# Decoder layer with eight routed experts: gate and up weights become the loaded operand and are fetched from DRAM once per tile of rows

## The reference

```python
logits = xt @ Ws + bs                       # 1600 x 8
topk_w, topk_idx = jax.lax.top_k(logits, K) # K = 2 of E = 8 experts
topk_w = jax.nn.softmax(topk_w, axis=-1)
g = jnp.einsum('td,edf->tef', xt, Wg)       # D = 256, F = 688
u = jnp.einsum('td,edf->tef', xt, Wu)
h = jax.nn.silu(g) * u
y = jnp.einsum('tef,efd->ted', h, Wd)
out = jnp.einsum('ted,te->td', y, combine)  # combine holds the two weights of a row
x = layernorm(x + out)
```

## Time and profile before

| | |
|---|---|
| three timed runs | 719.72 us median (718.25 to 720.38) |
| the profiled execution | 723.84 us, of which the span of the trace is 721.9 us |
| PE busy | 645.6 us (89%) in 5190 instructions |
| PEld busy | 494.8 us (69%) |
| DVE, ACT, POOL busy | 381.0, 315.6, 287.8 us |
| DMA | 73.95 MB, 102 GB/s over the span; q1 65.53 MB, q0 7.61 MB |
| granted TensorE clock | 0.951 of 2.4 GHz on the mean |

### The profile page before, as it was taken

How to read it: one execution, slowest core, us unless ns; L and a number is a source line. 1 busy time by engine, 2 the same in 40 slices (tenths; PEclk the granted TensorE clock), 3 DMA queues, 4 the chain that set the end, 5 groups by cost and what they waited for, 6 DMA issues and landing times. The chain is left out here.

```text
span 721.9 us, 15610 instructions
## 1 busy us (share of the span) xinstructions
PE 645.6 (89%) x5190; PEld 494.8 (69%) x5191; DVE 381.0 (53%) x975; ACT 315.6 (44%) x761; POOL 287.8 (40%) x522
## 2 busy tenths in 40 slices
PE   6988977999999989999899729999999999999960
PEld 5887855677777767777677516777777777777750
DVE  2878765777777866787677641222222222222214
ACT  2344333677777766777676512222222222222202
POOL 3435454433333376336742321334333333334323
PEclk9999986999999998999999958999999999999995
DMA  8232114455556556555555550111221122112205
GB/s 255 76 77 73 55 34 125 130 167 163 169 170 173 160 152 188 167 163 163 145 147 144 186 214 23 26 31 28 33 36 30 30 31 35 29 30 30 28 1 182
DMA packets 60831, 73.95 MB, mean 102 GB/s; under 512 B 9498, under 2 KB 50786, under 8 KB 60002
## 3 DMA queue, kind: packets, MB, share of 16 engines
q1 hardware_dynamic: 54626, 65.53, 30.7%
q0 software_dynamic: 6144, 7.61, 6.5%
HBM read 38.38 MB, written 12.44 MB: 70 GB/s over the span
## 5 line engine op out<-in xcount | busy, mean ns | idle before, releaser
L1443 DVE TENSOR_REDUCE cmx<-ps 100x1 f32<-100x361 f32 x256 | 134.5, 531 | 69.5 <-PE ps L956 65.2
L1233 ACT ACTIVATE cpr<-ps 128x300 f32<-128x300 f32 x256 | 104.7, 419 | 57.6 <-PE ps L967 57.0
L1739 POOL DMA_INDIRECT accd<-y,si x32 | 51.3, 1602 | 137.4 <-DVE y L1962 137.4
L1950 DVE TENSOR_TENSOR hh<-sg,ps 128x344 f32<-128x344 f32 x64 | 32.8, 513 | 113.5 <-PE ps L1811 113.5
L956 PE MATMUL ps<-st 96*100 96x361 bf16 x256 | 85.7, 338 | 6.5 <-DMA st<-parts 3.1
L1833 PE MATMUL ps<-WD,hT 128*128 x384 | 88.3, 380 | 1.4 <-DVE y L1962 0.7
L1811 PE MATMUL ps<-WG,xsT 128*128 x256 | 86.3, 460 | 0.6 <-ACT xsT L1867 0.6
L1811 PE MATMUL ps<-WU,xsT 128*128 x256 | 85.6, 457 | 0.0
L967 PEld LDWEIGHTS ps<-st 120*128 120x128 bf16 x768 | 62.8, 102 | 31.6 <-issue 8.8
L1833 PEld LDWEIGHTS ps<-WD,hT 128*128 128x128 f32 x384 | 72.8, 190 | 16.1 <-issue 1.9
L967 PE MATMUL ps<-st 120*128 120x100 bf16 x768 | 76.8, 208 | 3.3 <-ACT st L1238 1.6
(11 more groups left out here) (219 smaller groups left out, 1104.7 us busy)
## 6 DMA issues: line engine op xcount, KB each, us to landing
st<-parts SPq DMA_DIRECT2D x192, 115.2 KB, 2.5
WD<-in_wd SPq DMA_DIRECT2D x6, 1024.0 KB, 11.5
cx<-in_ctxT SPq DMA_DIRECT2D x16, 361.0 KB, 5.1
WG<-in_wg SPq DMA_DIRECT2D x8, 688.0 KB, 4.7
WU<-in_wu SPq DMA_DIRECT2D x8, 688.0 KB, 4.5
x_sb<-in_x SPq DMA_DIRECT2D x8, 200.0 KB
x1d<-x SPq DMA_DIRECT2D x8, 200.0 KB
x1Td<-x1T SPq DMA_DIRECT2D x8, 200.0 KB, 3.3
```

The lines of the kernel that those rows point to most:

```text
L1233: act.activation(pr[:, h % (2 * HG), :], ps[:, B_T + h % 2, 0:NCH * L], ACT.Exp).then_inc(exp_ok, 1)
L1443: dve.tensor_reduce(mx[:, half, hh:hh + 1], ps[0:L, B_S + h % 2, 0:CTX], AX_X, ALU.max).then_inc(max_ok, 1)
L1739: pool.indirect_dma_start(accd, bass.IndirectOffsetOnAxis(ap=si[:, t.par:t.par + 1], axis=0), y[:, t.par, :], None, compute_op=ALU.add, bo ...
L1950: dve.tensor_tensor(hh[:, t.par, f * FH:(f + 1) * FH], sg[:, f, :], ps[:, B_U + f, 0:FH], ALU.mult).then_inc(h_ok, 1)
```

## The change

1. `WG` and `WU` are no longer in SBUF as a whole. On the host the columns of gate and up of an expert are laid out as 11 blocks of 128 (`ORDER`, `GU` = 1408 columns): gate 0 to 3, gate 4, a block that holds the last 48 columns of gate and (from column 64) of up, up 4, and up 0 to 3. SP fetches them from DRAM for each tile (`weights(t)`), 1.44 MB a time (two runs of 5632 bytes a partition), into one of four buffers `W`. The fetch for tile t waits until the gate and up products of tile t-4 are made, and reads the tile's expert from `expert_of` first. The buffer `W0` is filled with expert 0 in the cross-attention; one more POOL instruction on `r_jv` makes sure that tile 0 is expert 0's.
2. In `gate_up` the weights are the loaded operand and `xsT` streams past them, 128 columns each: 11 blocks x 2 chunks = 22 products, 44 PE instructions. The result has the hidden columns on the partitions, as `down` wants them, so `turn_hidden` and the two copies of `hT` are gone. The blocks come in three parts of 4, 3 and 4, each with its own bank for even and odd tiles. ACT makes one silu of 512 columns and two of 128, DVE two products of 128 and one of 512, straight into `hT`.
3. `WD` is fetched in the batches 0 to 5 of the cross-attention, `W0` in batch 6, in place of the pieces of `WG` and `WU`. Nothing but the stores is issued in its last turn.
4. The last norm comes in five pieces of 2, 3, 3, 3 and 2 slots of 128 rows (the last slot has 64). The root is taken by ACT (with a table load ahead of it), the reciprocal and the shift by DVE, POOL has no part in it. ACT applies slots 0 to 8, DVE slots 9 to 12.

```diff
-FH = F // 2
 FC = (F + P - 1) // P
 FP = FC * P
+FULL = F // P
+FLEFT = F - FULL * P
+U_AT = 64
+ORDER = ((("g", 0), ("g", 1), ("g", 2), ("g", 3)), (("g", 4), ("both", 5), ("u", 4)), (("u", 0), ("u", 1), ("u", 2), ("u", 3)))
+GU = P * sum(len(part) for part in ORDER)
...
-NQ = 4
-QT = TP // NQ
+PIECES = ((0, 2), (2, 5), (5, 8), (8, 11), (11, TP + 1))
+NQ = len(PIECES)
...
-                    for n in range(2 * E):
-                        if i == (n if n < E else n - 1):
-                            W, w = ((WG, wg), (WU, wu))[n % 2]
-                            sp.dma_start(W[:, :, n // 2, :], w[n // 2, :, :].rearrange("(k p) f -> p k f", p=P))\
-                                .then_inc(experts_in, 16)
+                    if 0 <= i < FC:
+                        sp.dma_start(WD[:, i, :, :], wd[:, i, :, :]).then_inc(R.wd_in, 16)
+                    if i == FC:
+                        sp.dma_start(W0[:, :, :], wgu[0, :, :, :]).then_inc(R.wd_in, 16)
...
-                    if i == NB - 1:
-                        for u in range(2):
-                            sp.wait_ge(kq_in[u], 16 * SLOTS * NB)
-                        sp.wait_ge(t_mm, H * (NB - 1))
-                        load_down(range(FC // 2))
...
-                    if i == NB - 1:
-                        load_down(range(FC // 2, FC))
...
-        hh = sb("hh", [P, 2, FP])
+        sg = sb("sg", [P, 6 * P])
+        W = [W0, *(sb(f"W{u}", [P, KC, GU]) for u in range(1, 4))]
...
+        def bank(t, part):
+            return 3 * t.par + part
...
+                def weights(t):
+                    wait(sp, gu_mm, 3 * (t.n - 3))
+                    e = sp.value_load(expert_of[0:1, bass.ds(t.n, 1)], min_val=0, max_val=E - 1)
+                    sp.dma_start(W[t.slot][:, :, :], wgu[bass.ds(e, 1), :, :, :].rearrange("e p k f -> p (e k) f"))\
+                        .then_inc(w_in[t.slot], 16)
+
+                def emit(t, n):
+                    if n == -1:
+                        weights(t + 2)
+                    if n + 3 < TILES:
+                        weights(t + 3)
...
-                def gate_up(t, e, halves):
+                def gate_up(t, parts):
                     pe.wait_ge(xT_ev, t.n + 1)
-                    for f in halves:
-                        wait(pe, h_ok, 2 * t.n + f - 1)
-                        for bank, W in ((B_G, WG), (B_U, WU)):
+                    wait(pe, w_in[t.slot], 16 * (t.lap + (t.slot > 0)))
+                    for part in parts:
+                        if part == 0:
+                            wait(pe, sg_ok, 2 * t.n - 3)
+                        else:
+                            wait(pe, h_ok, 2 * t.n - 4 + part)
+                        for i, (kind, _) in enumerate(ORDER[part]):
+                            c = i + sum(len(p) for p in ORDER[:part])
                             for k in range(KC):
-                                mm = pe.matmul(ps[:, bank + f, 0:FH], xsT[:, t.par, k, :],
-                                               W[:, k, bass.ds(e, 1), f * FH:(f + 1) * FH],
-                                               start=(k == 0), stop=(k == KC - 1))
-                            mm.then_inc(gu_mm, 1)
-
-                def turn_hidden(t):
-                    pe.wait_ge(h_ok, 2 * t.n + 2)
-                    wait(pe, hTa_ev, t.n)
-                    wait(pe, hTb_ev, t.n)
-                    for c in range(FC):
-                        mm = pe.transpose(ps[:, B_H + c // 4, c % 4 * P:(c % 4 + 1) * P],
-                                          hh[:, t.par, c * P:(c + 1) * P], ident[:, :])
-                        if c in (3, FC - 1):
-                            mm.then_inc(hT_mm, 1)
+                                mm = pe.matmul(ps[:, bank(t, part), i * P:(i + 1) * P], W[t.slot][:, k, c * P:(c + 1) * P],
+                                               xsT[:, t.par, k, :], start=(k == 0), stop=(k == KC - 1))
+                        mm.then_inc(gu_mm, 1)
...
                     for c in range(FC):
                         if c == 0:
-                            pe.wait_ge(hTa_ev, t.n + 1)
-                        if c == 4:
-                            pe.wait_ge(hTb_ev, t.n + 1)
+                            pe.wait_ge(h_ok, 2 * t.n + 2)
...
-                        turn_hidden(t - 1)
                     if n + 1 < TILES:
-                        coming = expert(t + 1)
-                        gate_up(t + 1, coming, (0,))
-                    if n == 1:
-                        pe.wait_ge(R.wd_in, 16 * FC)
+                        gate_up(t + 1, (0,))
                     if n >= 1:
                         down(t - 1, leaving)
                     if n + 2 < TILES:
                         turn_rows(t + 2)
                     if n + 1 < TILES:
-                        gate_up(t + 1, coming, (1,))
+                        gate_up(t + 1, (1, 2))
...
+                def silus(t, part):
+                    act.wait_ge(gu_mm, 3 * t.n + part + 1)
+                    wait(act, h_ok, 2 * t.n - part)
+                    if part == 0:
+                        a = act.activation(sg[:, 0:4 * P], ps[:, bank(t, part), :], ACT.Silu)
+                    else:
+                        act.activation(sg[:, 4 * P:5 * P], ps[:, bank(t, part), 0:P], ACT.Silu)
+                        a = act.activation(sg[U_AT:U_AT + FLEFT, 5 * P:6 * P], ps[0:FLEFT, bank(t, part), P:2 * P], ACT.Silu)
+                    a.then_inc(sg_ok, 1)
...
+                def hidden(t, part):
+                    dve.wait_ge(sg_ok, 2 * t.n + (2 if part == 1 else 1))
+                    dve.wait_ge(gu_mm, 3 * t.n + part + 1)
+                    if part == 1:
+                        wait(dve, y_mm, t.n - 1)
+                        left = slice(U_AT, U_AT + FLEFT)
+                        dve.tensor_tensor(hT[:, t.par, FULL - 1, :], sg[:, 4 * P:5 * P], ps[:, bank(t, part), 2 * P:3 * P], ALU.mult)
+                        h = dve.tensor_tensor(hT[left, t.par, FULL, :], sg[left, 5 * P:6 * P],
+                                              ps[left, bank(t, part), P:2 * P], ALU.mult)
+                    else:
+                        h = dve.tensor_tensor(hT[:, t.par, 0:FULL - 1, :].rearrange("p c t -> p (c t)"), sg[:, 0:4 * P],
+                                              ps[:, bank(t, part), :], ALU.mult)
+                    h.then_inc(h_ok, 1)
...
+                deviation(0)
+                deviation(1)
+                apply(0, (0, 1)).then_inc(res_ok, 1)
+                deviation(2)
+                apply(1, (2, 3, 4)).then_inc(res_ok, 1)
+                deviation(3)
+                apply(2, (5, 6))
+                deviation(4)
+                apply(2, (7,)).then_inc(res_ok, 1)
+                apply(3, (8,)).then_inc(res_ok, 1)
...
-                    last_stats(q)
+                    sums_of(q)
+                    if q >= 1:
+                        scales(q - 1)
+                    moments(q)
+                    if q >= 1:
+                        shifts(q - 1)
+                normal(9)
+                normal(10).then_inc(scaled_ok, 1)
+                scales(NQ - 1)
                 dve.wait_ge(rstd_ok, NQ)
-                for j in slots(NQ - 1):
-                    r = dve.tensor_scalar(acc[:, j, :], acc[:, j, :], mv[:, j, 0:1], rstd[:, j:j + 1],
...
```

More of the change, by code:

```diff
@@ L1605, in _, with experts @@
                             apply(i - 1)
-        return WG, WU, WD
-def experts(nc, ps, ident, R, WG, WU, WD, x2d, accd, out):
+        return W0, WD
+def experts(nc, ps, ident, R, W0, WD, wgu, x2d, accd, out):
     with ExitStack() as ctx:
@@ L1692, in _ @@
                 R.store_weights(sp, 4, x2d)
+                sp.wait_ge(routed, 7)
+                def weights(t):
[8 more added lines that the diff above has]
+                        weights(t + 3)
+                steps(emit, sp)
                 sp.wait_ge(added, 16 * TILES)
@@ L1966, in emit, with sums_of @@
                     if n >= 1:
[L1967 to L1970 removed]
                         weigh(t - 1)
                     if n + 1 < TILES:
[L1973 removed]
+                        hidden(t + 1, 1)
+                        hidden(t + 1, 2)
                 steps(emit, dve)
[L1977 to L1981 removed]
+                def sums_of(q):
+                    dve.wait_ge(acc_ins[q], 32 if q == NQ - 1 else 16)
+                    for j in range(*PIECES[q]):
+                        m = dve.bn_stats(stats[0:rows(j), j, :], acc[0:rows(j), j, :])
@@ L1982, in last_stats, with moments @@
                     m.then_inc(mv_ok, 1)
-                    dve.wait_ge(mv_ok, 3 * q + 1)
-                    for j in slots(q):
-                        n = P if j else TR
-                        m = dve.bn_aggr(mv[0:n, j, :], stats[0:n, j, :])
+                def moments(q):
+                    dve.wait_ge(mv_ok, 2 * q + 1)
+                    for j in range(*PIECES[q]):
+                        m = dve.bn_aggr(mv[0:rows(j), j, :], stats[0:rows(j), j, :])
```

(36 more changed lines are left out.)

145 lines of the change are left out of this document (56 added, 89 removed).

## The result

The changed kernel takes 788.1 us (median of four runs, 781.4 to 789.9); the kernel before, on the same chip, takes 720.1 (718.3 to 720.9). The ratio is 1.093, with an interval of 1.086 to 1.100. The profiled execution took 789.93 us, its span is 788.0 and its mean granted clock 0.916 (before: 723.84, 721.9 and 0.951).

What follows compares the result with a forecast made beforehand. PE was taken as the bound, with the gather chain only 0.1 us behind. Terms -3.5 - 2.8 + 0.5 - 1.3 - 0.3 = -7.4 us took the profiled 723.84 to 716.4, as a median 712.3 us; range 703 to 735.

Steps and rivals of the forecast that it cites:

- d = 0.3: Experts' steps: delay of the gather by the weight fetch, taken as 0.3 us, bounded 0 to 2.5; steps -3.5 us.
- the same formula: Experts' steps: two waits for gathered rows in a row sum to C - W, so the mean step is (C + W)/2.
- C: Experts' steps: chain from the down products through y, add and gather to the rows PE turns; 8.0 us before, 8.3 forecast.
- Rival 1: Experts' steps: gather waits out the fetch, wait 2.8 us every second step, +25.7 us, 745 us; chance 0.15.
- Rival 2: Experts' steps: gather and fetch take turns piece by piece, delay about 1.2 us, +5.7 us, 725 us; chance 0.25.
- Rival 3: Experts' steps: gather doesn't bind, step is PE's 7.65 us, -18.7 us, 701 us; chance 0.08.
- Rival 4: Experts' steps: PE gets no faster, 0.116 us an instruction, -3.9 us, 716 us; inside the forecast, no chance of its own.
- W: Experts' steps: PE's work in a step, forecast at 7.78 us (7.65 to 7.90) against 8.10 before.
- End of the cross-attention, -2.8: Last batch's normalising no longer waits for batch 14's store behind WD: -2.8 us (bounds 0 and -3.2).
- Start of the stage, +0.5: Experts' first tile: products at the low clock, first gathers sharing engines with 4.3 MB of weights: +0.5 us.
- Last tiles, -1.3: Ahead of tile 30's down products, a turning of 0.66 us and a wait of 0.66 go: -1.3 us.
- Last norm, -0.3: Final norm: smaller first piece starts 0.5 to 0.8 us earlier, partly offset by added work: -0.3 us (-1.0 to +0.7).

Runs made afterwards that it cites:

- experiment 5: Changed kernel with POOL's gather for tile t+3 issued ahead of the add of tile t-1: 707.0 us, 0.981 of the kernel before.
- 8: Changed kernel with the gather ahead of the add and the fetch issued only once the gather of tile t+1 has landed: 706.8 us, 0.980 of the kernel before.
- experiment 6: Changed kernel with the fetch still one transfer but in pieces of 1408 bytes for 5632: 776.0 us, 1.076 of the kernel before.
- experiment 7: Kernel before with only the 1.44 MB fetch a step added, into a buffer nobody reads: 774.8 us, 1.075 of the kernel before.
- experiment 3: Changed kernel with each fetch issued as four transfers of 352 columns: 748.6 us, 1.041 of the kernel before.
- experiment 9: Changed kernel with each fetch issued as 11 transfers of 128 columns: 741.5 us, 1.030 of the kernel before.
- 10: Kernel before with only POOL's gather moved ahead of the add: 717.4 us, 0.997 of the kernel before.
- experiment 4: Changed kernel with the fetch issued only when the gather of tile t+1 has landed: 715.1 us, 0.991 of the kernel before.

## Why the prediction was wrong

**The step that failed** is "So I take d = 0.3", the delay of the gather by the fetch. The traces show 6.4 to 7.2 us to landing in every second step for 2.9; I take 7.0, d = 4.1. The upper bound of 2.5 failed as well: I let the gather wait for what was left of the fetch at the time its bytes were due, 6.4 to 8.9 us. It did wait for that, but the fetch was mis-sized: from its first bytes it takes 5.8 us on the median and not 3.4, and the fetch shown above moved bytes for 6.1 us, to 11.6 us after the down products. The row that I went by (the gather alone runs at half the engines' share) says how much room it leaves, not who goes first. When two queues meet, an unused share is no evidence that the smaller one gets it, and I should have given the gather's wait behind the fetch more than 0.15.

By the same formula, with d = 4.1, C is 12.1, the step (12.1 + 7.72)/2 = 9.9 us, and 29 of them are 51 us over the kernel before. Measured are 308.69/29 = 10.64 us and +72.0. The other 21 us come of a term that no part of the prediction had: the clock. I took PE's work for the same with and without a wait. Behind the 13 waits of 3.0 to 5.0 us the 44 instructions took 6.0 to 7.6 us instead of 4.91. Counted straight from PE's timeline, the 29 steps hold 55.1 us of waits for rows; without waits they take 224.0 us (experiments 5 and 8), which is 12.7 less than before. What remains, 308.7 - 224.0 - 55.1 = 29.6 us, is PE's own work at the slower clock. The formula has 63 us of waits, as it counts 14.5 of 4.4 us where there were 13 of 4.2 and one of 0.75: 8 us too much in one term hide part of the 29.6 that it lacks.

**The rivals.** Rival 1 had the mechanism: the place, the alternation of steps (short, 7.7, and long, 12.6 to 15.8) and the direction. Its price was too low for the two reasons above: a wait of 2.8 for 3.0 to 5.0, as the fetch lasts longer, and no clock. Rival 2 (piece by piece) took a piece for 5632 bytes. With the trace's 11264 (0.42 us) eight turns cost 3.4 us, so the late landings alone don't refute it. Experiment 6 does: in pieces of 1408 bytes (3.4/64 = 0.05 us) eight turns would cost 0.4 us, and the late gathers came 3.1 to 3.9 us late. For the add the turns are real (experiment 7). Rival 3's step of 7.65 is what experiments 5 and 8 reach nearly (7.72), by taking the gather out of the chain, not because DVE was freed. Rival 4 is refuted by the pace of the instructions.

The Trainium skill, "DMA: Bandwidth & Descriptors", section "Queues, rings and completion order", spoke against my choice, and the trace agrees in direction: a queue that got the engine keeps it for long. By its packet of 9 to 17 descriptors a fetch in four transfers should have let the gather in after at most the first of them; experiment 3 lands at up to 6.0 us, which is more than that. The gathers of experiment 6 were late by far more than 17 of its pieces of 0.05 us, and the add of experiment 7 got its turn after a single piece. Where the change-over is stays open, and so does why add and gather differ.

**What was right.** PE's work: 0.113 us an instruction predicted, 4.91/44 = 0.112 measured, W 7.72 for 7.78. The formula for the alternating wait: a wait by it of 12.1 - 7.72 = 4.4, where 3.0 to 5.0 were measured. The time of the collision: bytes of the fetch from 5.5 us after the down products (down products end at 535.5, bytes from 541.0). PE did not wait for weights. DVE's and ACT's new work is hidden, as the 7.72 us of the short step shows.

**End of the cross-attention, -2.8.** The last normalising follows its root within 0.1 us (0.2 was said), and from batch 14's to batch 15's it is 9.78 us for 12.19: -2.4. At the first gather's issue it is -3.2, measured from batch 14's (batch 14's at 403.92 and the gather at 423.64, for 406.85 and 429.76), close to what was said. The other 2.9 of the 6.1 in the table came before batch 14. The traces of the nine kernels with the changed code reach it anywhere from 400.9 to 406.7 us, those of the three with the code before from 404.4 to 406.9. So one pair of traces can't show a gain there.

**Start of the stage, +0.5**, was +3.4. The term "another 0.3 by the choice of d" is the same mistake. The first gathers share the engines with three fetches of weights, 4.3 MB, and PE turned the first rows at 430.98, 7.3 us after the first issue. Experiment 3, which divides these fetches into four as well, has 18.9 us in this stage, and experiment 9 20.5, for 23.2 here, so the loss goes with these fetches.

**Last tiles, -1.3**, was -0.8. From tile 29's down products to tile 30's are 5.72 us for 6.38: the turning and its wait are gone as said, but 28 gate and up instructions (3.13 us) stand there for 8 (2.31), which I left out.

**Last norm, -0.3**, was -2.4 (14.96 us for 17.36), below the bound of -1.0. The other kernels with the new norm have 14.9 to 16.2, experiments 7 and 10 with the old one 17.4 and 17.8, so it belongs to the norm. I didn't separate its parts (smaller first piece, five pieces, no hop through POOL), so which one gives it stays open.

## What to carry to other kernels

Before adding a stream of large transfers, look at which small transfers are on a chain and when they are issued against it. A small one behind a large one paid all that was left of the large one here, however idle the engines were on the mean. Then order them: hold the large one until the small one has landed (experiment 4), or take the small one out of the chain (experiment 5). Dividing the large one works too, until the issuing engine becomes the bound (0.81 us each, experiment 9). And a wait of some us on TensorE is to be priced with the slower clock behind it, which followed all 13 waits of 3.0 to 5.0 us here.

## What the runs showed of the hardware

- A gather of 135 KB lands in 2.8 to 2.9 us alone and in 6.4 to 7.2 behind a transfer of 1.44 MB from the other queue; in 4.5 to 5.5 behind 0.72 MB, in 2.8 to 3.4 beside 0.13 MB.
- A transfer of 1.44 MB that would take 3.4 us at 422 GB/s landed 6.9 us after its issue on the median. In the one shown the other engines were through by about 545.7 us, and one engine needed until 547.05 for its last pieces and the gather's between them. Why one engine is late stays open.
- An add that was under way when the fetch came took turns with it, packet by packet (experiment 7).
- The granted clock fell from 1.00 to 0.50 before the end of a wait of 4.5 us, and the next 44 instructions took 7.4 us for 4.91. Behind waits of 1.8 to 2.3 us they took 4.91 in some steps and 6.5 in others. In experiment 3 a wait of 1.87 us ahead of 516.60 was followed by 4.91 us (granted clock 1.00 from 517 to 523 us) and one of 1.92 us ahead of 551.99 by 6.54 (0.76 from 552 to 559).
- SP, issuing one transfer behind the other, needs 0.73 us for each (experiment 9; 0.81 with the reading of the expert's number between tiles), where a single one shows 0.35.
